# A router stage relieved: residual stored by the stage before, zeros written earlier, top eight taken tile by tile, and one sum of the attention weights per block

## The reference

```python
# softmax attention, 16 heads of 32
scores = jnp.einsum('bshd,bthd->bhst', q, k) / sqrt(dh) * spiral_weight
attn = jax.nn.softmax(scores, axis=-1)
x = x + (attn @ v) @ Wo.T + bo
# MoE: 64 experts, top 8, capacity 256
logits = x @ router_weight.T
topw, topi = jax.lax.top_k(jax.nn.softmax(logits), 8)
topw = topw / topw.sum(-1)
# each expert works on its first 256 tokens; y = sum of topw * expert(x)
```

## Time and profile before

| | |
|---|---|
| median of 3 runs | 5465.84 us (5462.49 to 5467.04) |
| profiled execution | 5482.55 us, its span 5480.8 us |
| TensorE busy | 4767.7 us (87%) |
| VectorE, ScalarE, GpSimd busy | 2394.7, 1611.4, 1534.5 us |
| mean granted TensorE clock | 0.930 of 2.4 GHz |

### The profile page before, as it was taken

One profiled execution on the slowest core, in us unless ns is written; L12 is line 12 of the kernel. 1 busy time (PEld: TensorE's weight loads), 2 busy tenths in 40 slices (PEclk: granted clock), 3 DMA queues, 4 the chain that ended last, 5 costly groups with the idle time before them and its releaser, 6 DMA issues. The chain is left out here.

```text
span 5480.8 us, 66367 instructions
## 1 busy us (share of the span) xinstructions
PE 4767.7 (87%) x26224; PEld 2542.8 (46%) x26224; DVE 2394.7 (44%) x3253; ACT 1611.4 (29%) x2716; POOL 1534.5 (28%) x953
## 2 busy tenths in 40 slices
PE   6048898799999999984999959999999989589996
PEld 3014343333333333243666636666666654456663
DVE  1783778456666666734222223333333321322222
ACT  2502555110555555822111122222222210121111
POOL 0011000100777776011555411111111110035553
PEclk9569999899999999987999979999999999689998
DMA  1000000100000000023999730000000022459997
GB/s 51 0 18 14 12 0 0 35 0 1 1 1 1 1 1 1 1 102 109 250 254 248 196 92 28 32 30 30 22 32 30 22 92 76 166 144 252 252 249 201
DMA packets 237100, 417.62 MB, mean 76 GB/s; under 512 B 30992, under 2 KB 119056, under 8 KB 236816
## 3 DMA queue, kind: packets, MB, share of 16 engines
q1 hardware_dynamic: 179472, 270.89, 14.3%
q0 software_dynamic: 57344, 142.64, 12.0%
HBM read 297.53 MB, written 115.93 MB: 75 GB/s over the span
## 5 line engine op out<-in xcount | busy, mean ns | idle before, releaser
L2208 PE MATMUL linb_pr_ps<-lin_z,linb_wt 128*128 128x512 f32 x1536 | 679.8, 596 | 16.3 <-POOL linb_slope_own L2178 16.3
L1384 ACT ACTIVATE attc_prob<-attc_ps 128x512 f32<-128x512 f32 x1024 | 548.9, 597 | 441.7 <-PE attc_ps L1295 440.9
L1408 DVE TENSOR_REDUCE attc_peak<-attc_ps 128x2 f32<-128x1024 f32 x384 | 469.6, 1225 | 256.4 <-PE attc_ps L1303 256.4
L1258 POOL TENSOR_TENSOR attc_acc<-attc_acc,attc_prob 128x2048 f32<-128x2048 f32 x120 | 547.9, 4566 | 118.4 <-ACT attc_prob L1384 106.2
L1295 PE MATMUL attc_ps<-att_q,att_k 32*128 32x512 f32 x2048 | 530.7, 617 | 0.0
L1303 PE MATMUL attc_ps<-att_k,att_q 32*128 32x512 f32 x1536 | 450.3, 663 | 0.0
L2208 PEld LDWEIGHTS linb_pr_ps<-lin_z,linb_wt 128*128 128x128 f32 x1536 | 287.2, 192 | 343.1 <-issue 326.5
L2384 DVE SCALAR_TENSOR_TENSOR linb_gated<-linb_osb,linb_norm_w,linb_proj 128x512 f32<-128x512 f32 x64 | 94.3, 1474 | 668.0 <-ACT linb_osb L2311 668.0
L2185 POOL TENSOR_TENSOR linb_sq<-linb_osb 128x512 f32<-128x512 f32 x64 | 70.0, 1094 | 1041.2 <-ACT linb_osb L2311 1041.2
L1316 PE MATMUL attc_ps<-attc_prob,att_v 128*32 128x256 f32 (+1 forms) x3472 | 315.0, 435 | 0.3 <-ACT attc_prob L1384 0.3
L933 DVE TENSOR_TENSOR_SCAN ssmb_state<-ssmb_decay,ssmb_bu 128x2048 f32<-128x2048 f32 x64 | 279.7, 4409 | 78.8 <-ACT ssmb_decay L880 78.8
(11 more groups left out here) (509 smaller groups left out, 7608.4 us busy)
## 6 DMA issues: line engine op xcount, KB each, us to landing
moe1w_wgu<-in_L_ffn_gate_up_proj SPq DMA_DIRECT2D x32, 1536.0 KB
moe2w_wgu<-in_L_ffn_gate_up_proj SPq DMA_DIRECT2D x32, 1536.0 KB
moe1w_wd<-in_L_ffn_down_proj SPq DMA_DIRECT2D x32, 512.0 KB
gated_features<-linb_gated SPq DMA_DIRECT2D x64, 256.0 KB
moe2w_wd<-in_L_ffn_down_proj SPq DMA_DIRECT2D x32, 512.0 KB
linc_gt<-gated_features SPq DMA_DIRECT2D x7, 2048.0 KB, 8.1
linb_wt<-in_L_attn_b_qkv_w SPq DMA_DIRECT2D x16, 768.0 KB
residual_rows<-residual SPq DMA_DIRECT2D x2, 4096.0 KB, 13.6
```

What stands on the lines that cost most here:

```text
L1258: pool.tensor_tensor(acc[:, n % 2, :, :], before, prob[:, U % NP, :, :], ALU.add).then_inc(pool_done, 2 if at == 1 else 1)
L1384: nc.scalar.activation(prob[:, U % NP, h, :], ps[:, n % 3 if at < 0 else at % 6, :], ACT.Exp).then_inc(exp_done, 1)
L1408: V.tensor_reduce(peak[:, w // TT % 2, i % QH, 2 * hp:2 * hp + 2, b], ps[:, bank:bank + 2, :], axis=AX.X, op=ALU.max).then_inc(mx_used, 1)
L2208: last = nc.tensor.matmul(pr_ps[:, use % 2, :], wt[:, b, kind, k, :], z[:, k, t * NB:(t + 1) * NB], start=(k == 0), stop=(k == DT - 1))
```

## The change

Five edits come together.

- In `attention_heads` SUMMED becomes (14, 15). The use "Z", its copy and `zsum` go; tiles 7 and 8 are added into `acc` like the others, and the reciprocal reads the sum in PSUM directly.
- X is stored to `residual_rows0` in four pieces of 1 MB by the stage before each router, each as soon as its four tiles are summed; that stage waits for all four.
- The zeros of `residual_rows1` are stored in ffn2 (for moe1) and in `linear_heads` (for moe2), in sixteen pieces, each stage with a memset on GpSimd.
- `moe_logits` has neither, so SP's queue holds the router's weights, z, the experts' weights.
- `max` and `match_replace` move from the head of `moe_routing` into VectorE's loop of `moe_logits`, one and two tiles behind the copy of the logits.

```diff
 project_and_add, and linear_outputs behind its last load:
+            for i in range(0, TT, 4):
+                sp.wait_ge(summed, i + 4)
+                sp.dma_start(g.y_dram[0][i * P:(i + 4) * P, :].rearrange("(i p) d -> p i d", p=P), g.X[:, i:i + 4, :]).then_inc(x_saved, 16)
+            sp.wait_ge(x_saved, 16 * (TT // 4))
 ffn (clear is True for ffn2):
+            if clear:
+                sp.wait_ge(blank, 1)
+                for i in range(TT):
+                    sp.dma_start(g.y_dram[1][i * P:(i + 1) * P, :], nothing[:, :]).then_inc(cleared, 16)
+                sp.wait_ge(cleared, 16 * TT)
...
+            pool.memset(nothing[:, :], 0.0).then_inc(blank, 1)
 attention_heads:
-        SUMMED = (7, 8, 14, 15)
+        SUMMED = (14, 15)
-                if done == SUMMED[1]:
-                    got.append("Z")
...
-                sources = [prob[:, (n - 1) % NP, :, :], prob[:, n % NP, :, :]]
-                if kind == "F":
-                    sem, count = summed_by(n - n % TT + POOLED[-1])
-                    pe.wait_ge(sem, count)
-                    sources.append(acc[:, n // TT % 2, :, :])
+                sem, count = summed_by(n - n % TT + POOLED[-1])
+                pe.wait_ge(sem, count)
+                sources = [prob[:, (n - 1) % NP, :, :], prob[:, n % NP, :, :], acc[:, n // TT % 2, :, :]]
...
-                if kind == "Z":
-                    dve.wait_ge(z_done, 2 * n + 1)
-                    V.tensor_copy(zsum[:, :], ps[:, bank, :]).then_inc(mx_used, 1)
-                    return
-                dve.wait_ge(z_done, 2 * n + 2)
-                dve.wait_ge(mx_used, use_at[U, "F"])
-                V.tensor_tensor(tot[:, :], ps[:, bank, :], zsum[:, :], ALU.add).then_inc(mx_used, 1)
+                dve.wait_ge(z_done, n + 1)
+                V.reciprocal(tot[:, :], ps[:, bank, :]).then_inc(mx_used, 1)
                 dve.wait_ge(mx_used, use_at[U, "F"] + 1)
-                V.reciprocal(tot[:, :], tot[:, :]).then_inc(sum_step, 1)
-                dve.wait_ge(sum_step, n + 1)
 moe_logits, SP:
-            sp.dma_start(g.y_dram[0][0:T, :].rearrange("(i p) d -> p i d", p=P), g.X[:, :, :]).then_inc(x_saved, 16)
-            sp.wait_ge(blank, 1)
-            for i in range(0, TT, NB_ROWS):
-                sp.dma_start(g.y_dram[1][i * P:(i + NB_ROWS) * P, :].rearrange("(i p) d -> p i d", p=P), nothing[:, :, :]).then_inc(x_saved, 16)
 moe_logits, VectorE:
-            for i in range(TT + NZ):
-                if i >= NZ:
+            for i in range(TT + NZ + 2):
+                if i >= NZ + 2:
+                    dve.wait_ge(top_done, i - NZ - 1)
+                    nc.vector.match_replace(others[:, i - NZ - 2, :], best[:, i - NZ - 2, :], logits[:, i - NZ - 2, :], -3.0e38).then_inc(others_done, 1)
+                if NZ + 1 <= i < TT + NZ + 1:
+                    dve.wait_ge(lg_used, i - NZ)
+                    nc.vector.max(best[:, i - NZ - 1, :], logits[:, i - NZ - 1, :]).then_inc(top_done, 1)
+                if NZ <= i < TT + NZ:
 moe_routing, VectorE:
-            for i in range(TT):
-                V.max(best[:, i, :], logits[:, i, :]).then_inc(chain, 1)
-            link.n = TT
-            for i in range(TT):
-                dve.wait_ge(chain, i + 1)
-                V.match_replace(others[:, i, :], best[:, i, :], logits[:, i, :], -3.0e38).then_inc(chain, 1)
 linear_heads, SP behind its first loads, and GpSimd's constants:
+            sp.wait_ge(consts, N_CONSTS)
+            for i in range(TT):
+                sp.dma_start(g.y_dram[1][i * P:(i + 1) * P, :], nothing[:, :]).then_inc(cleared, 16)
...
+            link(pool.memset(nothing[:, :], 0.0))
```

More of the change, by code:

```diff
@@ L204, in project_and_add @@
         y_ps = L.ps("y_ps", [P, NY, D])
-        loaded, y_ready, y_used, biased, summed = (L.sem(s) for s in ("loaded", "y_ready", "y_used", "biased", "summed"))
+        loaded, y_ready, y_used, biased, summed, x_saved = (
+            L.sem(s) for s in ("loaded", "y_ready", "y_used", "biased", "summed", "x_saved"))
         block = L.block()
@@ L648, in ffn @@
         y_ps = L.ps("y_ps", [P, 2, D])
+        nothing = L.sb("nothing", [P, D])
+        blank, cleared = L.sem("blank"), L.sem("cleared")
         loaded, z_ready, zt_done, zt_ready, y_ready, y_used, biased, summed, passed = (
@@ L1505, in load_pair, with moe_logits @@
                 sp.dma_start(wd_tail[x * TAIL:(x + 1) * TAIL, r, :], wd_dram[P:IN, 2 * j + x, :]).then_inc(w_loaded[r], 16)
-        with nc.sbuf_tensor(f"{name}_logits", [P, TT, E_N], F32) as logits:
-            moe_logits(nc, g, name + "a", logits, load_pair)
-            moe_routing(nc, g, name + "b", logits, index)
+        with ExitStack() as ctx:
+            logits, others = (ctx.enter_context(nc.sbuf_tensor(f"{name}_{n}", [P, TT, E_N], F32)) for n in ("logits", "others"))
+            best = ctx.enter_context(nc.sbuf_tensor(f"{name}_best", [P, TT, TOP], F32))
+            moe_logits(nc, g, name + "a", logits, best, others, load_pair)
+            moe_routing(nc, g, name + "b", logits, best, others, index)
         moe_experts(nc, g, name + "c", index, wgu, wd, wd_tail, w_loaded, load_pair, last)
-def moe_logits(nc, g, name, logits, load_pair):
+def moe_logits(nc, g, name, logits, best, others, load_pair):
     NZ = 4
-    NB_ROWS = 4
     with Layer(nc, name) as L:
@@ L1519, in moe_logits @@
         z = L.sb("z", [P, NZ, D])
-        nothing = L.sb("nothing", [P, NB_ROWS, D])
-        blank = L.sem("blank")
         zt = L.sb("zt", [P, 2, D])
@@ L1527, in moe_logits @@
         lg_ps = L.ps("lg_ps", [P, 2, NB])
-        z_ready, zt_done, zt_ready, lg_ready, lg_used, rw_loaded, rwt_done, rwt_ready, x_saved = (
-            L.sem(s) for s in ("z_ready", "zt_done", "zt_ready", "lg_ready", "lg_used", "rw_loaded", "rwt_done", "rwt_ready", "x_saved"))
+        z_ready, zt_done, zt_ready, lg_ready, lg_used, rw_loaded, rwt_done, rwt_ready = (
+            L.sem(s) for s in ("z_ready", "zt_done", "zt_ready", "lg_ready", "lg_used", "rw_loaded", "rwt_done", "rwt_ready"))
+        top_done, others_done = L.sem("top_done"), L.sem("others_done")
         z_saved = [L.sem(f"z_saved{b}") for b in range(NZ)]
@@ L1548, in _ @@
                 sp.wait_ge(z_saved[b], 16 * (TT // NZ))
-            sp.wait_ge(x_saved, 16 * (1 + TT // NB_ROWS))
-        @block.gpsimd
-        def _(pool):
-            pool.memset(nothing[:, :, :], 0.0).then_inc(blank, 1)
         @block.vector
@@ L1607, in _, with moe_routing @@
                 nc.scalar.copy(zt[:, i % 2, :], zt_ps[:, i % 2, :]).then_inc(zt_ready, 1)
-def moe_routing(nc, g, name, logits, index):
+def moe_routing(nc, g, name, logits, best, others, index):
     with Layer(nc, name) as L:
@@ L1616, in moe_routing @@
         QP = EP // GE
-        best = L.sb("best", [P, TT, TOP])
-        others = L.sb("others", [P, TT, E_N])
         share = L.sb("share", [P, TT, E_N])
@@ L2403, in linear_outputs @@
         ss_ps = L.ps("ss_ps", [P, NB])
-        (ones_ready, ss_done, ms_ready, rms_ready, inv_ready, y_done, y_used, taken, summed) = (
-            L.sem(s) for s in ("ones_ready", "ss_done", "ms_ready", "rms_ready", "inv_ready", "y_done", "y_used", "taken", "summed"))
+        (ones_ready, ss_done, ms_ready, rms_ready, inv_ready, y_done, y_used, taken, summed, x_saved) = (
+            L.sem(s) for s in ("ones_ready", "ss_done", "ms_ready", "rms_ready", "inv_ready", "y_done", "y_used", "taken", "summed", "x_saved"))
         w_loaded = [L.sem(f"w_loaded{j}") for j in range(4)]
@@ L2485 @@
     1: lambda nc, g: lru(nc, g),
-    2: lambda nc, g: ffn(nc, g, "ffn1"),
+    2: lambda nc, g: ffn(nc, g, "ffn1", False),
     3: lambda nc, g: ssm(nc, g),
-    4: lambda nc, g: ffn(nc, g, "ffn2"),
+    4: lambda nc, g: ffn(nc, g, "ffn2", True),
     5: lambda nc, g: attention(nc, g),
```

28 lines of the change are left out of this document (12 added, 16 removed).

## The result

The kernel after takes 5414.2 us (median of 4 runs, 5406.9 to 5420.2), the one before 5464.2 (4 runs, 5461.7 to 5467.0). The ratio is 0.9909, 95% interval 0.9895 to 0.9923: 50 us less, with 42 to 57 inside the interval, where 33 were forecast (5433). The four runs of after are 5406.9, 5408.8, 5419.6 and 5420.2, so the median lies between two groups and no run took it. The profiled execution of after has a span of 5418.5 us at a mean granted clock of 0.933.

What follows compares the result with a forecast made beforehand. Bound read stage by stage: GpSimd's additions in attention's first twelve blocks, VectorE at block boundaries, the SP queue in the logits stages. Terms sum to 33.0 us off the 5465.8 median: 5433, range 5410 to 5458; likeliest case (0.45) 5419 to 5446.

Steps and rivals of the forecast that it cites:

- Early sum, 1 us: Attention's first twelve blocks: removal frees 1.72 us a block on TensorE, but GpSimd's additions leave only 0.1; 1 us saved.
- Reciprocal, 7 us: Attention block boundaries: VectorE's chain loses the addition before the reciprocal; 0.65 us at each of 11 boundaries, 7 us saved.
- VectorE beside GpSimd: Attention: the tensor_tensor ending the split of the maxima meets a GpSimd addition; 0.2 us a block lost, -2 us.
- Rival 3: Attention: VectorE's tensor_tensor waits behind a whole GpSimd addition, 1.5 us a block, 18 us more; 5451 us, chance 0.20.
- Last four blocks, 6.5 and 0.7 us: Attention's last four blocks: ScalarE regains 1.62 us each, 6.5 us; the very last block's chain ends 0.7 earlier.
- Logits stages, 6.4 and 12.4: Both logits stages: VectorE no longer stalls for z stores, weights issue earlier; 6.4 and 12.4 us saved at low clock.
- rival 1: Clock rises in the logits stages, at most 11.8 us more each, or GpSimd is not the bound; 5418 us, chance 0.18.
- Routing, 10.5: Start of each routing stage: the VectorE work that moves away takes 5.26 us each; 10.5 us saved.
- Store tail, -9.0: Stage before each router: it waits 4.5 us for the last 1 MB of the residual to land; twice, -9.0 us.
- Rival 2: Stage before each router: the store tail is 13.6 us, not 4.5, twice 9.1 us more; 5451 us, chance 0.10.
- Zeros and memset, -0.5: ffn2 and linear heads: zero stores are hidden; TensorE waits for half of a 0.95 us memset, -0.5 us.
- Rival 4: Attention: VectorE's wait passes to TensorE in full, 4.5 us in each of 12 blocks; slower, 5487 us, chance 0.07.

Runs made afterwards that it cites:

- experiment 5: The kernel after, but each sum is first copied out of PSUM and the reciprocal taken from the copy; 5427.1 us, ratio 0.9932.
- experiment 6: The kernel after with GpSimd relieved: ones written instead of its first addition, the others adding two of four heads (timing only); 5387.9 us, ratio 0.9853.
- experiment 10: The kernel after with expert weight loads issued by the routing stage, and only block 11's sum copied out of PSUM before its reciprocal; 5383.7 us, ratio 0.986.
- experiment 11: As experiment 10, plus 7 added matmuls behind the last tile before each router and 2 ahead of the router's weights; 5379.9 us, ratio 0.9838.
- after again: The kernel after, unchanged, profiled a second time; span 5405.3 us.
- before again: The kernel before, unchanged, profiled a second time; span 5457.9 us.
- experiment 1: The kernel before with the attention edit alone; 5443.1 us, ratio 0.9952.
- experiment 9: The kernel after with weight loads issued by the routing stage, plus unread matmuls before each router, ahead of its weights and inside the logits stages; 5398.9 us, ratio 0.9882.
- experiment 12: As experiment 11, plus one added matmul of 256 columns after every two tiles in the logits stages; 5391.2 us, ratio 0.9866.

## Why the prediction was right, and where it was not

The measured time is 19 us under the forecast. It lies inside the range of 5410 to 5458, and outside the likeliest case's own (5419 to 5446). The mechanism held in most parts; the largest part of what came on top, the spared drops of the clock in attention (11.7 us), stood in no term, and another 6 us of the median are executions whose logits stage happened to run faster. That these stayed small enough for the range is luck. Point by point:

- **Early sum, 1 us.** Right, rather nothing: 67.6 us a block with and without it (before and experiment 5), and 1.7 us a block once GpSimd is out of the way (experiment 6). The step "of 1.72 only 0.1 remains" held, and it is what a count of removed instructions would have missed by 20 us.
- **Reciprocal, 7 us.** 0.65 a boundary was 0.7, together 7.7. Two things were missing. The bank that is freed later, with bounds taken for 11 boundaries, costs nothing there but 2.6 at the twelfth, where all uses share one bank (experiment 10). And the shorter wait at each boundary spares clock drops: 17.7 less 6.0 is 11.7 us, the largest thing that the sum lacked. (In the trace of experiment 11 the same code spared only 7.4.) The chain was read from one boundary, and the block lengths of before (67.6 to 70.7) were never asked why they differ.
- **VectorE beside GpSimd, -2 us.** The meeting costs VectorE 0.8 us a block, and the block lengths leave no room for it on the path, so nothing. The instruction that waits was the cast, which the prediction had only in its third rival, not the tensor_tensor. (The Trainium skill, "SBUF — State Buffer", who interferes with whom, lists casts among those that can take the pair shared with GpSimd, and the 0.99 us agree with that; the 4.49 us agree with the part on two inputs.) Rival 3 did not come in after: the exponentials of the last tiles wait for GpSimd, so the two engines keep step, and the cast always comes 0.9 to 1.1 us before an addition ends. With 0.7 us more on the chain it fell out of step once.
- **Last four blocks, 6.5 and 0.7 us.** Two blocks got 1.6 each and the last one 2.5, its end included; the first got nothing and paid 2.8 (the bank). So 3.0 of the 7.2 came.
- **Logits stages, 6.4 and 12.4.** 6.1 and 13.3, at the low clock that was assumed. In after again the second stage gave 10 more, with the clock up: the first half of rival 1 (11.8 at most, 9.8 measured) comes true in some executions, which makes most of the two groups. The second half, that GpSimd is not the bound, is refuted by experiments 5 and 6.
- **Routing, 10.5.** 5.3 and 6.0, 11.3 together (3.7 and 6.0 against before again, whose first routing stage was 1.6 shorter).
- **Store tail, -9.0.** 4.5 and 4.5, exactly that; 1 MB landed in 4.3 us where the line between 256 KB and 4 MB gave 4.6. Rival 2 is out.
- **Zeros and memset, -0.5.** TensorE waits 17.0 us for the constants instead of 16.3: -0.7. The sixteen stores lay hidden in both places.
- **Rival 4.** Not met: a tensor_tensor of 4.49 us came in one block of one experiment only.

Without the stalls of the first profile, before (5457.9 again) and after (5418.5) differ by 39.4 us: attention 22.9, logits 19.4, routing 9.7, less 9.0 and 1.6 for tails and linear heads; that is 41.4, and the 2.0 lost again lie in other stages, 1.4 of it ahead of attention (where experiment 1 has it too). The medians come to 50 because that execution of before took 4.5 us less than the median of before, and because the executions of after with a faster logits stage put its median 6.0 under the profiled one.

## What to carry to other kernels

When engines wait for each other around a loop, removing work from the one that looks busiest can give nothing, and a shorter link in another's chain its whole length (here 0 of 1.72 us and all of 0.72); read which wait ends last at the boundary. If equal blocks differ in length, look at the granted clock of each before counting anything: short waits of TensorE were here worth more through the clock (11.7 us) than by themselves (7.7). Profile a kernel a second time before explaining a difference in a stage that the change doesn't touch.

## What was not expected of the hardware

- In after, a 128x16 cast from fp32 to bf16 on VectorE took 0.96 to 1.13 us instead of 0.20 while GpSimd added from SBUF, and ended with GpSimd's instruction; a tensor_tensor as small took 4.49 us in the same place (experiment 5).
- At one boundary TensorE was busy 6.27 of 8.90 us and 6.8 us at 1.2 GHz followed, at another 7.25 of 8.20 and 3.4 us followed; other boundaries with the same waits had no drop. A stage of transposes and 64-column products ran at 2.4 GHz throughout (0.99 to 1.00) when TensorE had worked up to its start (experiments 9, 11 and 12). When it had stood still for 9 us the mean over the stage was anything from 0.50 to 0.84, and which of them differed between executions of one kernel (0.50 and 0.76 for the second stage of after).
- TensorE issued single instructions 0.7 to 1.4 us apart for some 7 us, with no wait in the profile, in one of fourteen profiled executions (19 us in two places). Where it comes from was not found.
